# Early-fusion embedding on one core: the text encoder's four layers laid out as one pipeline, and the image pipeline one stage deeper

## The reference

```python
# _L0_tok_ref: x (64,128,64,3), per sample
h = layernorm(x.reshape(b, t, j * 3), ln0_g, ln0_b).reshape(b, t, j, 3)
h = relu(conv2d(h, conv1_w, conv1_b, ((2, 2), (1, 1))))
h = layernorm(h.reshape(b, t, j * 3), ln0_g, ln0_b).reshape(b, t, j, 3)
h = relu(conv2d(h, conv2_w, conv2_b, ((2, 2), (0, 0))))
h = layernorm(h.reshape(b, t, j * 2), ln1_g, ln1_b).reshape(b, t, j, 2)
h = relu(conv2d(h, conv3_w, conv3_b, ((2, 2), (0, 0))))        # 256 channels
return layernorm(res, ln1_g, ln1_b) @ out_w + out_b             # (64,128,64)
# _L0_txt_ref: 64 texts of 77 tokens, D=64, L=4 layers, H=8 heads of 8
for i in range(L):
    q = x @ Wq[i] + bq[i];  k = v = x @ Wv[i] + bv[i]
    o = softmax(q k^T * scale) v            # per head
    x = x + layer_norm(o @ Wo[i] + bo[i], ln1_g[i], ln1_b[i])
    h = gelu(x @ W1[i] + b1[i]);  x = x + layer_norm(h @ W2[i] + b2[i], ln2_g[i], ln2_b[i])
return layer_norm(x, fin_g, fin_b)
# then over the 205 joined rows of each sample
h = h + attention(layernorm(h));  h = h + gated_experts(layernorm(h))
```

## Time and profile before

| what | value |
|---|---|
| median of 3 runs (lowest, highest) | 2704.18 us (2699.97, 2717.02) |
| the profiled execution's own time | 2723.24 us |
| its span, first to last instruction | 2721.4 us |
| mean granted TensorE clock | 0.904 of full speed |
| busy: PE / DVE / ACT / POOL | 83% / 67% / 49% / 44% |
| image stage, with its setup | 0 to 536 us |
| text setup, text layers, final norm and next setup | to 576 us, to 1750 us, to about 1800 us |
| joint attention, experts | to about 2330 us, to the end |

### The profile page before, as it was taken

One profiled execution on the slowest core, in us unless ns is written; L12 is line 12 of the kernel. 1 busy time (PEld: TensorE's weight loads), 2 busy tenths in 40 slices (PEclk: granted clock), 3 DMA queues, 4 the chain that ended last, 5 costly groups with the idle time before them and its releaser, 6 DMA issues. The chain is left out here.

```text
span 2721.4 us, 62098 instructions
## 1 busy us (share of the span) xinstructions
PE 2250.7 (83%) x19897; PEld 1805.2 (66%) x19897; DVE 1816.3 (67%) x5614; ACT 1344.1 (49%) x3116; POOL 1207.3 (44%) x1523
## 2 busy tenths in 40 slices
PE   5699999768886888778977888448888899699998
PEld 5699999656665766666765666436666676466665
DVE  3355565367755677467755775568888865588888
ACT  2122222125544555545554554557666655566663
POOL 2233333225546555655554554654444432443442
PEclk8899999869988999889887998759999955699999
DMA  5100000000000000000000000000000000000000
GB/s 124 29 12 17 12 17 6 1 1 1 0 1 1 1 0 0 0 2 0 0 1 1 1 0 1 0 1 0 0 0 0 0 0 1 4 10 9 8 9 11
DMA packets 39551, 19.18 MB, mean 7 GB/s; under 512 B 29508, under 2 KB 38852, under 8 KB 39366
## 3 DMA queue, kind: packets, MB, share of 16 engines
q1 hardware_dynamic: 39466, 18.00, 2.7%
HBM read 14.63 MB, written 3.36 MB: 7 GB/s over the span
## 5 line engine op out<-in xcount | busy, mean ns | idle before, releaser
L456 PE MATMUL im_c<-im_a_hi,im_w 128*128 128x256 f32 (+2 forms) x1920 | 429.4, 318 | 46.8 <-POOL im_a_lo L353 46.8
L456 PEld LDWEIGHTS im_c<-im_a_hi,im_w 128*128 128x128 f32 x1920 | 321.4, 191 | 63.3 <-POOL im_a_lo L353 47.6
L1064 POOL TENSOR_TENSOR tx_KB<-tx_KF,tx_head_rows 128x1248 fp32r<-128x1248 f32 x128 | 288.0, 2270 | 48.7 <-DVE tx_KF L932 48.7
L456 PE MATMUL im_c<-im_a_lo,im_w 128*128 128x256 f32 (+2 forms) x960 | 304.1, 317 | 0.0
L874 POOL TENSOR_TENSOR tx_rstd<-tx_var_eps,tx_power 77x4 f32<-77x4 f32 x128 | 130.7, 1021 | 369.6 <-DVE tx_var_eps L870 369.0
L1135 ACT ACTIVATE tx_PT<-tx_scores_t 77x624 f32<-77x624 f32 x256 | 175.3, 685 | 163.5 <-PE tx_scores_t L1278 154.1
L1278 PE MATMUL tx_scores_t<-tx_QP,tx_KB 128*77 128x78 f32 x2048 | 201.4, 250 | 9.9 <-DVE tx_QP L952 4.2
L946 DVE TENSOR_REDUCE tx_mpad<-tx_scores 77x8 fp32r<-77x616 f32 x256 | 202.3, 790 | 6.5 <-PE tx_scores L1260 5.9
L346 POOL TENSOR_TENSOR im_rstd<-im_var_eps,im_power 128x4 f32<-128x4 f32 x64 | 68.6, 1073 | 305.0 <-DVE im_var_eps L274 305.0
L1278 PEld LDWEIGHTS tx_scores_t<-tx_QP,tx_KB 128*77 128x77 f32 x2048 | 183.1, 157 | 29.5 <-DVE tx_QP L952 29.4
L456 PEld LDWEIGHTS im_c<-im_a_lo,im_w 128*128 128x128 f32 x960 | 182.7, 190 | 8.4
(11 more groups left out here) (312 smaller groups left out, 5977.7 us busy)
## 6 DMA issues: line engine op xcount, KB each, us to landing
im_x<-x SPq DMA_DIRECT2D x16, 384.0 KB, 3.3
out<-h_img SPq DMA_DIRECT2D x32, 64.0 KB
tx_toks<-x_txt SPq DMA_DIRECT2D x1, 1925.0 KB
im_raw<-L_tok_conv_w SPq DMA_DIRECT2D x1, 1280.0 KB, 8.9
out<-h_txt SPq DMA_DIRECT2D x32, 38.5 KB
im_raw<-L_tok_conv_w SPq DMA_DIRECT2D x1, 960.0 KB, 4.7
im_raw<-L_tok_conv_w SPq DMA_DIRECT2D x1, 640.0 KB, 6.1
tx_raw_W<-L_txt_W SPq DMA_DIRECT2D x2, 256.0 KB, 5.8
```

Of the source, the lines that this page charges most:

```text
L456: last = pe.matmul(acc[:, :, d0:d1], w[c][:, slot, part], img[:, b0_:b1_, d0 + shift:d1 + shift, kj:kj + J], start=opens, stop=closes)
L1064: pool.tensor_tensor(KB[:, par, t], KF[:, t].bitcast(F32).unsqueeze(1).broadcast_to([P, HPT, QW]), head_rows[:].unsqueeze(2).broadcast_to( ...
```

## The change

The image stage gets one step more of depth: in a step PE does the first convolution of quad n, the second of n-1, the third of n-2, and the output of n-3. `a_hi` and `a_lo` get two buffers each for all convolutions. SP issues the loads of the later stages at step U-2 (14 of 16).

The text stage loses both loops over quads and layers. One Python list of N+5 = 69 steps (N = 4 layers x 16 quads) is written out on each engine; a step holds every kind of operation once for each quad, each with its own lag (`n`, `n - 1`, ... `n - 5`), so attention and feed-forward of different quads stand in the same step, and quads of the next layer follow those of the last without a phase between. Weights are read straight from `w_all`; the copies to `w` are gone. `up` and `down` move to the two `work` banks, which now have twelve users in a step (`WORK`), and PE waits for the last reader of a bank before it takes it (`take`). Attention and feed-forward get norm tiles of their own. The end of the second norm is changed from a product with the deviation, a product with the gain and a sum to a product with the gain and four scalar-tensor-tensor sums. All semaphore values are constants.

```diff
-            step(0, 0, True, False)
-            step(1, 1, False, False)
-            if U > 4:
-                with eng.Fori(1, U // 2 - 1) as i:
+        def each_quad(eng, step):
+            for n in range(-1, 4):
+                step(n, n % 2)
+            with eng.Fori(2, U // 2 - 1) as i:
+                step(i * 2, 0)
+                step(i * 2 + 1, 1)
+            for n in range(U - 2, U + 3):
+                step(n, n % 2)
...
-                def step(n, par, first, last):
-                    if not last:
-                        if not first:
-                            sp.wait_ge(normed_ready, (n * 3 - 2) * QUAD)
-                        load(n + 1, 1 - par)
-                    if first:
-                        for inputs in later_loads:
-                            inputs.load(sp)
+                def step(n, par):
+                    if here(n + 2):
+                        if past(n + 1):
+                            sp.wait_ge(normed_ready[0], n * QUAD + QUAD)
+                        load(n + 2, par)
+                    if isinstance(n, int) and n == U - 2:
+                        for inputs in later_loads:
+                            inputs.load(sp)
...
-                def step(n, par, first, last):
-                    cuts = cuts_before(n)
-                    two_before = not isinstance(n, int) or n > 1
-                    conv(0, par, 1 if first else n * 3 - 1, n, (lambda: project(n - 2)) if two_before else None)
-                    if not first:
-                        conv(2, 0, cuts, n - 1)
-                    conv(1, 0, cuts + (1 if last else 2), n)
-                    if not first:
-                        turn_res(n - 1)
-                    if last:
-                        project(n - 1)
-                        conv(2, 0, cuts + 2, n)
-                        turn_res(n)
-                        project(n)
+                def step(n, par):
+                    if here(n):
+                        first_conv(n, par, 0)
+                    if here(n - 3):
+                        turn_res(n - 3)
+                    if here(n):
+                        first_conv(n, par, 1)
+                    if here(n - 3):
+                        project(n - 3)
+                    if here(n - 1):
+                        second_conv(n - 1, 1 - par)
+                    if here(n - 2):
+                        third_conv(n - 2, par)
...
+        WORK = dict(x=1, k0=0, k1=1, q0=0, q1=1, v=1, o=0, a=0, f=1, up0=0, up1=1, y=0)
+        def bank(use):
+            return work[WORK[use]]
...
-        def end_sum(dve, n, par, g, m):
-            dve.wait_ge(y_scaled, n + 1)
-            dve.tensor_tensor(yn[:, par], yn[:, par], of("ln2_g"), ALU.mult).then_inc(y_gain, 1)
-            dve.wait_ge(y_gain, m + 1)
-            dve.wait_ge(shifted, n + 1)
-            dve.tensor_tensor(quads(g), yn[:, par], x_shift[:, par], ALU.add).then_inc(x_new, 1)
+                def scale_y(q):
+                    if live(q):
+                        dve.wait_ge(y_squared, q + 1)
+                        if q >= 2:
+                            dve.wait_ge(x_new, q - 1)
+                        dve.tensor_tensor(y_yn[:, q % 2], in_rows("y"), of(q, "ln2_g"), ALU.mult).then_inc(y_scaled, 1)
...
+                def sum_y(q):
+                    if live(q):
+                        dve.wait_ge(y_power, q + 1)
+                        dve.wait_ge(y_shifted, q + 1)
+                        dve.wait_ge(y_scaled, q + 1)
+                        for b in range(QUAD):
+                            last = dve.scalar_tensor_tensor(out=quads(q)[:, b], in0=y_yn[:, q % 2, b],
+                                                            scalar=y_rstd[:, q % 2, b:b + 1], in1=y_shift[:, q % 2, b],
+                                                            op0=ALU.mult, op1=ALU.add)
+                        last.then_inc(x_new, 1)
...
+                def step(n):
+                    find_max(n - 2, 2)
...
+                    normalise_o(n - 2, 0)
+                    sum_y(n - 5)
+                    cut_k(n, 1)
+                    sum_a(n - 4)
...
-                set_attention_weights(0)
-                set_cols(0)
-                set_feed_forward_weights(0)
-                set_rows(0)
+                dve.memset(PT[:], 0.0).then_inc(outs_cleared, 1)
+                for rows_split in (xs, xs_f, os_):
+                    dve.memset(rows_split[:].bitcast(F32), 0.0).then_inc(outs_cleared, 1)
+                for n in range(N + 5):
+                    step(n)
...
+                def step(n):
+                    cut_f(n - 5)
+                    shift_a(n - 3)
+                    split_k(n - 1, 1)
+                    shift_y(n - 5)
+                    cut_x(n)
+                    split_k(n - 1, 0)
+                    power_a(n - 4)
+                    cut_o(n - 3)
+                    power_y(n - 5)
...
+                def step(n):
...
+                    lo_q(n - 1, 0)
+                    gelu(n - 5, 1)
+                    gelu(n - 5, 0)
+                    copy_outs(n - 3, 3)
+                    exp(n - 2, 0)
...
+                def take(use, read, q):
+                    k = WORK[use]
+                    if held[k]:
+                        pe.wait_ge(*held[k])
+                    held[k] = (read, q + 1)
+                    return work[k]
...
+                def step(n):
+                    weigh(n - 3, 2)
+                    turn_f(n - 5)
...
+                    down(n - 5)
...
+                pe.wait_ge(outs_cleared, 5)
+                for n in range(N + 5):
+                    step(n)
```

1326 lines of the change are left out of this document (637 added, 689 removed).

## The result

The changed kernel took 2446.67 us (median of 4 executions, 2403.27 to 2487.36), beside 2710.6 us (2699.97 to 2734.61) for the kernel before: 0.890 of the time, 95% interval 0.877 to 0.903. Predicted were 2443 us and 0.9036. The profiled execution took 2426.08 us, its span is 2424.3 us.

The account below looks back on a forecast made before the run. PE was taken as busiest, idle at image ends and in text phases. From a 2721.4 us span, 28 (images), 1 (setup) and 233.6 us (texts) came off: 2458.8 span, 0.9036, median 2443 us; range 2385 to 2570.

Parts of the forecast that it names:

- I take 1.0 us: half of what waits cost before: Text step: PE's waits add 1.0 us to its floor of 13.34 us; before, they cost 2.2 us a quad.
- T = 14.3: Forecast time in us of one full step of the merged text pipeline, range 13.6 to 15.2; forecast's chance .56.
- rival B: Text step: waits vanish, 13.4 us a step at the floor, and short filling (80 us); median 2376 us; chance .13.
- PE's largest waits ahead of L1259: Expected sign in the text trace: PE waits most at `tx_work0` before L1259, ended by DVE.
- the walk of the lists: Going through a text step's four engine lists: two tight places, DVE's chain before `tx_work0` (0.3 to 1.3 us) and a queued exp.
- Filling and draining: Text stage's first five and last five steps: 94 us taken, between 72 and 143, plus 3 us for the clock.
- With one step more between a norm and its convolution: Image stage: three PE waits for `a_lo` go, 32.9 us; net gain for images 28 us, range 15 to 40.
- The cover of the late loads: Moved loads are out by about 440 us, text setup starts at about 508 us: some 65 us to spare.
- C: Text step: ACT's table loads fall on the path through exp, 16.3 us a step; median about 2560 us; chance .17.
- D: Text step: straight-line instructions arrive too slowly for PE, some 1 us a step, 15.3 us; about 2510 us; chance .07.
- E: Text step: PE's work banks become a ring of waits with ACT and DVE; slower than before, 2704 us and more; chance .04.
- break-even of 18.8: Text step time in us at which the changed kernel would be no faster than before, 4.5 us over the forecast.

## Why the prediction came out right, and where it was wrong

The forecast came out right: the mechanism in the texts was the one that was costed, and 262.6 us of gain in the span were forecast where 297.1 were measured (2458.8 and 2424.3 us). That the medians agree within 4 us (2443 and 2446.67) is luck, since the four executions behind the second spread over 84 us; like for like the forecast was 34.5 us too long (0.9036 of the time, just outside the interval that was measured), by terms that were off in both directions:

| term | forecast | measured |
|---|---|---|
| text: 59 full steps | 14.3 us each, 844 | 13.41 us each, 791 |
| text: filling, draining, low clock | 97 | 117 |
| images and text setup | -29 | -19.1 |
| the other stages | 0 | -11.9 |

**The step.** Its floor was read rightly (PE, then ACT and DVE close behind), but the term for what the waits cost above it ("I take 1.0 us: half of what waits cost before") was mis-sized, and so T = 14.3: rival B's 13.4 is what was measured. PE is busy 12.93 us, not 13.34, since the busy time of before counts short groups whose fill now overlaps with other work (argued, not shown), and idle 0.48 us: 0.34 for the gelu, 0.14 ahead of L1259. The place was right, though the sign that the prediction named for it, PE's largest waits ahead of L1259, did not come: the chain behind `tx_work0` is just closed, with 0.14 us between L933 and PE, and lengthening it by 0.86 us costs 0.62. What the walk of the lists lacked is that a chain which ends 0.3 to 1.3 us late by estimates that each have a few tenths of error may as well end in time.

**Filling and draining** were 117 us where 97 were taken, within the stated 72 to 143. The low clock, costed at 3 us, can be nearly all of the difference: PE worked 38 us at clock 0.50 at the two ends (0.74 in the first 68 us, 0.73 in the last 55), which at clock 1.00 would be 19 us less by my estimate.

**The images.** The step that failed is "With one step more between a norm and its convolution, the waits of 6.35, 23.16 and 3.35 us for `a_lo` have a whole quad's PE work before them: 32.9 us go." The waits did go, but 23.16 of them go by the move of the loads alone (535.8 to 512.5 us), and not by depth: with the early loads depth makes it 17 us worse. What depth itself does away with over late loads in the old order, 9.7 us of waits, it more than gives back in the tail: two waits of 4.7 to 5.0 us, foreseen, and about 6 us of low clock behind them, mis-sized (I took 1 us for each). Of the 6 us that were to come back from the low clock of the head, about 3 did: PE worked 12.5 us at clock 0.50 in the first 113 us before, and 6.0 us after. The cover of the late loads was as reckoned: SP issues them from 354.77 to 421 us, and the text setup starts at 519.

**The other stages** were rightly costed at nothing. Their 11.9 us are 13.8 us of the attention, at clock 0.86 in the one profile and 0.90 in the other, less 1.9 us elsewhere.

**The rivals.** C (table loads on PE's path) is refuted by the run without them, 0.14 us a step. Its figure was also summed short: with the 65.6 us for one us of T that the prediction gives, T = 16.3 is a median of about 2573, not 2560. The loads of this kernel take 1.28 us each; the instruction ahead of one ends 0.02 us before it, and the function behind starts 0.01 us after it. The Trainium skill, "ScalarE: Activation LUTs", what ACT_TABLE_LOAD costs, gives about 1.28 us for the load and about 1.4 us of drain on top, 2.7 us a switch. The trace agrees on the load and doesn't show the drain: without the 123 loads ACT worked 601.3 us in the text stage where it had worked 764.0, which is 1.32 us less for each.

D (straight-line code) does not show: PE is busy 96% in the full steps, and the 0.34 us wait has a named releaser. E (the ring of banks) did not happen. In small, its mechanism is in the run with the longer chain, where PE waits 0.77 us in each step for a bank that DVE has still to read. In large, a loop of waits between PE and ACT can undo the whole gain: two loads more took the text stage to 1217.5 us, 43 us longer than that of the kernel before. There the loop ran through the results of the gelu and of `down`; no wait for a bank is listed. Its step of 18.4 us lies under the prediction's break-even of 18.8, which holds filling at 97 us; with the prediction's own 65.6 us for one us of T it would be 18.3. Contention between DVE and GpSimd stayed out at the sums, as forecast: both groups take 0.86 us, and GpSimd has nothing ready while they run.

## What to carry to other kernels

Test each part of a change alone before crediting the one with the better story: here a line that moves DMA issues out of the way of the next input did all that an extra pipeline stage was thought to do. In a pipeline over phases, half of the gain can come from never emptying it, and a good part of that is TensorE's clock. A wait of 5 us in a full stretch cost its length and then some at the low clock, so in a tail put ready work ahead of a transpose that waits. When an added operation is hidden on an engine that is not the bound, ask how far the next one would be: one pair of table loads cost 0.14 us a step, the second pair, with the order that it brought, 4.8 us.
